# A gated cross-attention and FFN kernel whose key side runs one group further ahead

## The chip, the cores and the metric

One NeuronCore of a Trainium2 chip. The metric is the device time of one execution in microseconds (us), as the median of several runs. Engines: TensorE (PE; its weight loads are PEld), VectorE (DVE), ScalarE (ACT), GpSimd (POOL) and SyncE (SP), which issues most transfers. Every engine works through its own queue in order and waits on semaphores.

## What is computed

Sixteen batches of 128 rows x 256 features, with one attention head:

```
Q = layernorm(x) @ Wq.T + bq          K = ctx @ Wk.T + bk
P = softmax(mask(Q @ K.T))            over the 128 rows of ctx, no scaling
x1 = x + tanh(g_xattn) * (P @ ctx @ Wo.T + bo)
y  = layernorm(x1) @ sign(weights).T * scale + bias,  clipped to +-100
out = x1 + tanh(g_ffn) * y
```

All is float32. Inputs x and ctx are [16, 128, 256], weights 256 x 256.

## The kernel before, in words

Two batches form a group (GB = 2), so there are eight groups (G = 8), 0 to 7. The query and key weights are multiplied once, so that a group needs the scores of normalised x against K = ctx (WkWq) only, and Z = ctx Wo^T takes the place of V. For a group the work is:

- TensorE transposes ctx into `ps_cT` and normalised x into `ps_xT` (`transpose_ctx`, `transpose_x`, L454, four each).
- ScalarE casts `ps_cT` to `cT_hi` (L183), and VectorE takes the rest as `cT_lo` (L360). ScalarE copies `ps_xT` to `xT` (L187).
- TensorE makes K and Z, each as 12 matmuls of hi and lo parts (`project_K`, `project_Z`, L459). ScalarE evicts them (L193, L198).
- TensorE makes the scores: one matmul adds the mask (L515), then four write the products (L520). VectorE takes the negated maximum (`nmax`, L370), ScalarE the exponentials (L204). TensorE transposes P (L528) into the same PSUM bank, ScalarE evicts it (L209), and `attend` multiplies it by Z (L539).
- VectorE turns `ps_O` into x1 (`residual`, L380), takes its statistics (`stats_x1`, L352, L356). TensorE transposes x1, ScalarE and VectorE split it (L213, L365), and `ffn` multiplies it by the sign weights (L459). VectorE scales (L388), GpSimd adds the bias and clips (L299, L303), VectorE adds x1 (`final`, L393), SyncE stores.

GpSimd also normalises x (`norm_x`, L281) from rstd and offset, made for units of one or two groups (`UNITS`, `offsets_x`, L266 to L272) from VectorE's statistics (`stats_x`, L342, L346), adds the output bias to x (`add_bo`, L293), and makes the rstd of x1 (`rstd_1s`, L286, L288).

The order on every engine is written out by hand, one loop over steps i on each. Nothing is scheduled at run time. In step i TensorE takes the scores of group i, the transposes of group i+1, x1 of group i-1, Z of group i, K of group i+1, P^T of group i, FFN of group i-1 and attend of group i. Ahead of the loop stand the combined weights and group 0's transposes and K. In step 0 the transposes of the centred sign weights (`w_cent`) stand in the place of the FFN. `cT_hi`, `cT_lo`, `xT`, `K_sb`, `Z_sb`, `p_sb` and `PT_sb` have two buffers, `xn` three; every PSUM tile has one.

Of the kernel before, what the change touches and what calls it, by code (L numbers as in the profile page):

```python
# [5 lines left out]
ALU = mybir.AluOpType  # L6
ACT = mybir.ActivationFunctionType
AX = mybir.AxisListType
F32 = mybir.dt.float32
F32R = mybir.dt.float32r  # L10
# [3 lines left out]
P = 128  # L14
# [7 lines left out]
def gated_xattn_ffn(nc, x, ctx, mask, g_xattn, g_ffn, wq, bq, wk, bk, wo, bo, w_ffn, scale_ffn, bias_ffn, out):  # L22
# [8 lines left out]
    DC = D // P  # L31
# [10 lines left out]

    UNITS = [(0, 2), (2, 4), (4, 8), (8, 12), (12, 16)]

    STATS_AT = {0: (2, 3), 1: (4, 5), 2: (6,), 3: (7,)}
    unit_of = lambda g: next(n for n, (lo, hi) in enumerate(UNITS) if lo <= g * GB < hi)

    with ExitStack() as stack:
        def sb(name, shape, dt=F32):
            return stack.enter_context(nc.sbuf_tensor(name, shape, dt))  # L50
# [30 lines left out]

        xn = sb("xn", [P, 3, GB, D])
        xT = sb("xT", [P, 2, DC, T])
        cT_hi, cT_lo = sb("cT_hi", [P, 2, DC, T], F32R), sb("cT_lo", [P, 2, DC, T], F32R)
        K_sb = sb("K_sb", [P, 2, DC, T])
        Z_sb = sb("Z_sb", [P, 2, GB, D])
        p_sb, PT_sb = sb("p_sb", [P, 2, GB, P]), sb("PT_sb", [P, 2, GB, P])
# [83 lines left out]
        def _(act):  # L171
# [8 lines left out]

            def evict_cT_hi(g):
                act.wait_ge(cT_prod, g + 1)
                nc.scalar.copy(cT_hi[:, g % 2], ps_cT).then_inc(cT_hi_done, 1)  # L183

            def evict_xT(g):
                act.wait_ge(xT_prod, g + 1)
# [44 lines left out]
            evict_xT(0)  # L231
            act.wait_ge(ps_bi_ready, 1)
            nc.scalar.activation(bi_g[:], o_bank[:, D:2 * D], ACT.Identity, scale=tanh_g[:, 1:2]).then_inc(bi_g_ready, 1)
            for i in range(G + 1):
                if i + 1 < G:
                    evict_cT_hi(i + 1)
                if i < G:
                    exp(i)
                if i >= 1:
                    evict_x1T_hi(i - 1)  # L240
                if i + 1 < G:
                    evict_xT(i + 1)
                if i < G:
                    evict_Z(i)
                    evict_PT(i)
                if i + 1 < G:
                    evict_K(i + 1)
                if i == 0:
                    act.wait_ge(ps_wT_ready, 1)
                    nc.scalar.copy(wT[:], ps_x1T).then_inc(wT_ready, 1)  # L250

        @block.gpsimd
        def _(pool):
# [63 lines left out]
                                    channel_multiplier=1).then_inc(mask_ready, 1)  # L317
            offsets_x(1)
            norm_x(1)
            pool.wait_ge(bo_g_ready, 1)  # L320
            for i in range(G + 2):
                if i < G:
                    add_bo(i)
                if i == 2:
                    pool.wait_ge(bi_g_ready, 1)
                    pool.wait_ge(clip_ready, 2)
                if i >= 2:
                    bias_and_clip(i - 2)
                if i + 2 < G:
                    if unit_of(i + 2) != unit_of(i + 1):  # L330
                        offsets_x(unit_of(i + 2))
                    norm_x(i + 2)
                if 1 <= i <= G:
                    rstd_1s(i - 1)

        @block.vector
        def _(dve):
# [19 lines left out]

            def split_cT(g):
                dve.wait_ge(cT_hi_done, g + 1)
                nc.vector.tensor_tensor(cT_lo[:, g % 2], ps_cT, cT_hi[:, g % 2].bitcast(F32), ALU.subtract  # L360
                                        ).then_inc(cT_lo_done, 1)

            def split_x1T(g):
# [38 lines left out]
            for c in range(DC):  # L402
# [13 lines left out]
            dve.wait_ge(woT_hi_ready, 1)  # L416
            nc.vector.scalar_tensor_tensor(out=woT_lo[:], in0=ps_Z, scalar=tanh_g[:, 0:1], in1=woT_hi[:].bitcast(F32),
                                           op0=ALU.mult, op1=ALU.subtract).then_inc(woT_lo_ready, 1)
            for i in range(G + 2):
                if 1 <= i <= G:  # L420
                    residual(i - 1)
                if i < G:
                    max_of_scores(i)
                if i >= 2:
                    scale_ffn_out(i - 2)
                if i == 0:
                    dve.wait_ge(w_loaded, 16)
                    nc.vector.tensor_scalar(w_sign2[:], w_sb[:], 0.0, 2.0, ALU.is_ge, ALU.mult).then_inc(sign2_done, 1)
                    dve.wait_ge(sign2_done, 1)
                    nc.vector.tensor_reduce(w_sum[:], w_sign2[:], AX.X, ALU.add).then_inc(w_sum_done, 1)  # L430
                if i + 1 < G:
                    split_cT(i + 1)
                if i == 0:
                    dve.wait_ge(w_sum_done, 1)
                    nc.vector.tensor_scalar(w_mean[:], w_sum[:], 1.0 / D, None, ALU.mult).then_inc(w_mean_done, 1)
                    dve.wait_ge(w_mean_done, 1)
                    for c in range(DC):
                        nc.vector.tensor_scalar(w_cent[:, c], w_sign2[:, c], w_mean[:, c:c + 1], None, ALU.subtract
                                                ).then_inc(w_cent_ready, 1)
                if 1 <= i <= G:  # L440
                    stats_x1(i - 1)
                    split_x1T(i - 1)
                for g in STATS_AT.get(i, ()):
                    stats_x(g)
                if i >= 2:
                    final(i - 2)

        @block.tensor
        def _(pe):
# [32 lines left out]
            def project_K(g):  # L482
                pe.wait_ge(cT_lo_done, g + 1)
                if g >= 1:
                    pe.wait_ge(K_done, DC * g)
                else:
                    pe.wait_ge(wqk_lo_ready, 1)
                for m in range(DC):
                    pairs = []
                    for c in range(DC):  # L490
                        w_hi, w_lo = (w[:, c, m * P:(m + 1) * P] for w in (wqk_hi, wqk_lo))
                        pairs += [(w_hi, cT_hi[:, g % 2, c]), (w_hi, cT_lo[:, g % 2, c]), (w_lo, cT_hi[:, g % 2, c])]
                    last = accumulate(ps_K[:, m], pairs)
                last.then_inc(K_prod, 1)

            def project_Z(g):
                if g >= 1:
                    pe.wait_ge(Z_done, g)
                else:
                    pe.wait_ge(woT_lo_ready, 1)  # L500
                for b in range(GB):
                    pairs = []
                    for c in range(DC):
                        c_hi, c_lo = (t[:, g % 2, c, b * P:(b + 1) * P] for t in (cT_hi, cT_lo))
                        pairs += [(c_hi, woT_hi[:, c]), (c_hi, woT_lo[:, c]), (c_lo, woT_hi[:, c])]
                    last = accumulate(ps_Z[:, b], pairs)
                last.then_inc(Z_prod, 1)

            def scores(g):
                if g >= 1:  # L510
                    pe.wait_ge(PT_done, g)
                else:
                    pe.wait_ge(tanh_ready, 1)
                    pe.wait_ge(mask_ready, 1)
                nc.tensor.matmul(ps_S_both, ones_b[:], mask_sel[:, g].rearrange("p b k -> p (b k)"), start=True, stop=False)  # L515
                pe.wait_ge(xT_done, g + 1)
                pe.wait_ge(K_done, DC * (g + 1))
                for b in range(GB):
                    for c in range(DC):
                        last = nc.tensor.matmul(ps_S[b], xT[:, g % 2, c, b * P:(b + 1) * P],  # L520
                                                K_sb[:, g % 2, c, b * P:(b + 1) * P], start=False,
                                                stop=(b == GB - 1 and c == DC - 1))
                last.then_inc(S_prod, 1)

            def transpose_p(g):
                pe.wait_ge(p_done, GB * (g + 1))
                for b in range(GB):
                    last = nc.tensor.transpose(ps_PT[:, b], p_sb[:, g % 2, b], ident[:])  # L528
                last.then_inc(PT_prod, 1)
# [48 lines left out]
            transpose_x(0)  # L578
            pe.wait_ge(kbias_ready, 1)
            nc.tensor.matmul(o_bank[:, D:2 * D], ones_1[:], bi_row[:], start=True, stop=True).then_inc(ps_bi_ready, 1)  # L580
            for i in range(G + 1):
                if i < G:
                    scores(i)
                if i + 1 < G:
                    transpose_ctx(i + 1)
                if i >= 1:
                    transpose_x1(i - 1)
                if i + 1 < G:
                    transpose_x(i + 1)
                if i < G:  # L590
                    project_Z(i)
                if i + 1 < G:
                    project_K(i + 1)
                if i < G:
                    transpose_p(i)
                if i == 0:
                    pe.wait_ge(w_cent_ready, DC)
                    transposes(ps_x1T, w_cent).then_inc(ps_wT_ready, 1)
                else:
                    ffn(i - 1)  # L600
                if i < G:
                    attend(i)


# [25 lines left out]
```

## Time and profile before

| | us |
|---|---|
| median of 3 runs | 91.12 (89.64 to 91.77) |
| the profiled execution | 89.64, span 87.9 |
| TensorE busy | 74.0 (84%) |
| its weight loads | 66.5 (76%) |
| GpSimd busy | 58.7 (67%) |
| VectorE busy | 51.4 (58%) |
| ScalarE busy | 36.6 (42%) |

The span is what the profile shows from first to last record; the time of the execution is 1.74 us more. Busy shares are means over the whole span. In this kernel the first 18 us (loads and weights) and the last 12 (one group's way to the output) differ from the rest, so the stretches are read one by one. An idle engine matters only where another waits for it. The chain of waits gives matmuls the time until the next one starts, while the list of instructions gives each its full latency, so the same piece has a somewhat shorter time, and a start up to 0.1 us later, in the chain.

### The profile page before, as it was taken

The page shows a single profiled execution, that of the slowest core. Times are in us where ns is not written, and L with a number is a line of the kernel's source. Part 1 is how long each engine was busy: PE and PEld are TensorE (multiplying, and loading weights), DVE is VectorE, ACT ScalarE, POOL GpSimd, SP SyncE. Part 2 cuts the span into 40 slices and gives each one's busy share as a digit, 9 for nine tenths or more (in the row PEclk, how much of TensorE's full clock was granted, in tenths as well). Part 3 has the DMA queues.
Part 4 walks back from the last instruction along what each step waited for, and adds up shares of the span by engine and source line. Part 5 has one row for each costly group of instructions (what it writes and reads, how often), then busy time and mean ns, then how long its engine had stood idle before and what let it go on. Part 6 is the DMA issues. An engine that isn't in the chain of part 4 may idle for free.

```text
span 87.9 us, 1571 instructions
## 1 busy us (share of the span) xinstructions
PE 74.0 (84%) x528; PEld 66.5 (76%) x528; DVE 51.4 (58%) x151; ACT 36.6 (42%) x98; POOL 58.7 (67%) x105
## 2 busy tenths in 40 slices
PE   2993999989999999999999999999999996725000
PEld 2992778968979989997997999799799895514000
DVE  0039007509945947983993892596389078495330
ACT  0060306458356651951755395095257517020000
POOL 5000884592079970888999698899999909658740
PEclk9999858999999999999999999999999999999655
DMA  2899999900000000003003003000300300110303
GB/s 15 307 324 366 348 348 348 329 11 0 0 0 0 0 0 0 11 0 127 0 0 119 0 7 118 1 0 0 119 7 0 119 0 0 65 54 0 119 0 119
DMA packets 7697, 7.44 MB, mean 85 GB/s; under 512 B 775, under 2 KB 7434, under 8 KB 7690
## 3 DMA queue, kind: packets, MB, share of 16 engines
q1 hardware_dynamic: 7216, 7.08, 25.2%
q10 hardware_dynamic: 474, 0.27, 1.1%
q8 instruction: 4, 0.07, 0.3%
q14 instruction: 3, 0.02, 0.1%
HBM read 5.25 MB, written 2.10 MB: 84 GB/s over the span
## 4 chain that ended last, share of the span: by engine, by line
PE 68%; DVE 8%; DMA 5%; POOL 5%; ACTq 4%; issue 3%; ACT 2%; POOLq 1%; DVEq 0%
PE ps_K L459 17%; PE ps_S L520 10%; PE ps_Z L459 9%; PE ps_O L539 8%; PE ps_F L459 8%; DMA bi_row<-in_L_ffn_bias_dram 5%; PE ps_cT L454 4%; PE ps_x1T L454 3%; PE ps_xT L454 3%; POOL f_biased L299 3%; DVE f_scaled L388 2%; PE ps_S L528 2%; PE ps_S L515 2%; DVE cT_lo L360 1%; ACT K_sb L193 1%
## 5 line engine op out<-in xcount | busy, mean ns | idle before, releaser
L299 POOL TENSOR_TENSOR f_biased<-f_scaled,bi_g 128x256 f32<-128x256 f32 x16 | 11.4, 735 | 8.2 <-DVE f_scaled L388 8.2
L380 DVE SCALAR_TENSOR_TENSOR x_sb<-ps_O,recip_p,xb_sb 128x256 f32<-128x256 f32 x16 | 7.0, 479 | 12.3 <-PE ps_O L539 10.1
L293 POOL TENSOR_TENSOR xb_sb<-x_sb,bo_g 128x256 f32<-128x256 f32 x16 | 11.3, 729 | 0.0
L183 ACT CAST cT_hi<-ps_cT 128x512 fp32r<-128x512 f32 x8 | 4.7, 586 | 15.5 <-PE ps_cT L454 15.5
L459 PE MATMUL ps_F<-wT,x1T_hi 128*128 128x256 f32 x32 | 8.6, 303 | 2.3 <-DVE x1T_lo L365 2.3
L266 POOL TENSOR_SCALAR ve_x<-mv_x 128x4 f32<-128x4 f32 (+1 forms) x5 | 1.5, 292 | 12.9 <-DVE mv_x L346 12.8
L281 POOL TENSOR_SCALAR xn<-x_sb,rstd_x,off_x 128x256 f32<-128x256 f32 x16 | 9.7, 614 | 0.5
L459 PE MATMUL ps_Z<-woT_hi,cT_hi 128*128 128x256 f32 x32 | 9.6, 299 | 0.0
L520 PE MATMUL ps_S<-K_sb,xT 128*128 128x128 f32 x64 | 9.3, 288 | 0.3 <-ACT xT L187 0.3
L459 PE MATMUL ps_K<-cT_hi,wqk_hi 128*128 128x256 f32 x32 | 9.2, 287 | 0.2
L459 PE MATMUL ps_K<-cT_hi,wqk_lo 128*128 128x256 f32 x32 | 9.0, 282 | 0.0
L459 PE MATMUL ps_K<-cT_lo,wqk_hi 128*128 128x256 f32 x32 | 9.0, 282 | 0.0
L520 PEld LDWEIGHTS ps_S<-K_sb,xT 128*128 128x128 f32 x64 | 7.7, 191 | 1.5 <-ACT xT L187 0.7
L459 PE MATMUL ps_Z<-woT_lo,cT_hi 128*128 128x256 f32 x32 | 8.9, 277 | 0.0
L459 PE MATMUL ps_Z<-woT_hi,cT_lo 128*128 128x256 f32 x32 | 8.9, 277 | 0.0
L539 PE MATMUL ps_O<-Z_sb,PT_sb 128*128 128x256 f32 x32 | 8.3, 382 | 0.0
L459 PEld LDWEIGHTS ps_F<-wT,x1T_hi 128*128 128x128 f32 x32 | 6.0, 188 | 2.8 <-DVE x1T_lo L365 2.8
L459 PE MATMUL ps_F<-wT,x1T_lo 128*128 128x256 f32 x32 | 8.0, 282 | 0.0
L393 DVE TENSOR_TENSOR out_sb<-f_clip,x_sb 128x512 f32<-128x512 f32 x8 | 5.5, 692 | 3.8 <-POOL f_clip L303 3.8
L388 DVE SCALAR_TENSOR_TENSOR f_scaled<-ps_F,rstd,sc_g 128x256 f32<-128x256 f32 x16 | 7.0, 476 | 0.9 <-POOL rstd L288 0.9
L193 ACT ACTIVATE K_sb<-ps_K,kbias 128x256 f32<-128x256 f32 x16 | 6.7, 477 | 1.2 <-PE ps_K L459 1.2
L204 ACT ACTIVATE p_sb<-ps_S,nmax 128x128 f32<-128x128 f32 x16 | 5.8, 369 | 2.5 <-DVE nmax L370 2.5
(90 smaller groups left out, 194.5 us busy)
## 6 DMA issues: line engine op xcount, KB each, us to landing
ctx_sb<-in_ctx_dram SPq DMA_DIRECT2D x8, 256.0 KB, 6.6
x_sb<-in_x_dram SPq DMA_DIRECT2D x8, 256.0 KB, 6.4
out_dram<-out_sb SPq DMA_DIRECT2D x8, 256.0 KB, 2.1
wk_sb<-in_L_xattn_Wk_dram ACTq DMA_DIRECT2D x1, 256.0 KB, 3.9
wq_sb<-in_L_xattn_Wq_dram SPq DMA_DIRECT2D x1, 256.0 KB, 3.7
wo_sb<-in_L_xattn_Wo_dram SPq DMA_DIRECT2D x1, 256.0 KB, 4.8
w_sb<-in_L_ffn_weights_dram SPq DMA_DIRECT2D x1, 256.0 KB, 5.6
bq_col<-in_L_xattn_bq_dram ACTq DMA_DIRECT2D x1, 1.0 KB, 4.5
```

The lines of the kernel that those rows point to most:

```text
L193: nc.scalar.activation(K_sb[:, g % 2, c], ps_K[:, c], ACT.Identity, bias=kbias[:, c:c + 1]).then_inc(K_done, 1)
L204: nc.scalar.activation(p_sb[:, g % 2, b], ps_S[b], ACT.Exp, bias=nmax[:, r:r + 1], accum_out=psum_p[:, r:r + 1]).then_inc(p_done, 1)
L281: nc.gpsimd.tensor_scalar(xn[:, g % 3, b], x_sb[:, r], rstd_x[:, r:r + 1], off_x[:, r:r + 1], ALU.mult, ALU.add).then_inc(xn_done, 1)
L293: nc.gpsimd.tensor_tensor(xb_sb[:, r], x_sb[:, r], bo_g[:], ALU.add).then_inc(xb_done, 1)
L299: nc.gpsimd.tensor_tensor(f_biased[:, r], f_scaled[:, r], bi_g[:], ALU.add).then_inc(f_biased_done, 1)
L380: nc.vector.scalar_tensor_tensor(out=x1_sb[:, r], in0=ps_O[:, b], scalar=recip_p[:, r:r + 1], in1=xb_sb[:, r], op0=ALU.mult, op1=ALU.add). ...
L388: nc.vector.scalar_tensor_tensor(out=f_scaled[:, r], in0=ps_F[:, b], scalar=rstd_1[:, r:r + 1], in1=sc_g[:], op0=ALU.mult, op1=ALU.mult).t ...
L393: nc.vector.tensor_tensor(out_sb[:, rows(g)], f_clip[:, g % 2], x1_sb[:, rows(g)], ALU.add).then_inc(out_done, 1)
L454: last = nc.tensor.transpose(dst[:, c, b * P:(b + 1) * P], src[:, b, c * P:(c + 1) * P], ident[:])
L459: last = nc.tensor.matmul(dst, lhsT, rhs, start=(n == 0), stop=(n == len(pairs) - 1))
L520: last = nc.tensor.matmul(ps_S[b], xT[:, g % 2, c, b * P:(b + 1) * P], K_sb[:, g % 2, c, b * P:(b + 1) * P], start=False, stop=(b == GB - ...
L539: last = nc.tensor.matmul(ps_O[:, b], PT_sb[:, g % 2, b], Z_sb[:, g % 2, b], start=True, stop=True)
```

## The change

TensorE makes the scores of group 0, the transposes of group 1 and K of group 1 ahead of its loop. In step i it then takes the scores of group i+1, the transposes and K of group i+2, and, as before, Z, P^T and attend of group i and x1 and FFN of group i-1. The other engines' loops follow. `cT_hi` and `cT_lo` have three buffers. The scores of group g wait for the eviction of P^T of group g-2, and P^T of group i waits until the exponentials of group i+1 have read the bank. VectorE's statistics of x for groups 2 and 3 come ahead of the loop, and GpSimd normalises x one group further ahead. In the last step (i = 7) P^T comes first, then Z, x1 of group 6 and attend; the FFN of group 6, x1 and FFN of group 7 follow. In the last round VectorE splits x1 before its statistics.

```diff
-    STATS_AT = {0: (2, 3), 1: (4, 5), 2: (6,), 3: (7,)}
+    STATS_AT = {0: (4,), 1: (5,), 2: (6, 7)}
...
-        cT_hi, cT_lo = sb("cT_hi", [P, 2, DC, T], F32R), sb("cT_lo", [P, 2, DC, T], F32R)
+        cT_hi, cT_lo = sb("cT_hi", [P, 3, DC, T], F32R), sb("cT_lo", [P, 3, DC, T], F32R)
...
ScalarE
+            exp(0)
+            evict_cT_hi(1)
+            evict_xT(1)
+            evict_K(1)
             for i in range(G + 1):
+                if i + 2 < G:
+                    evict_cT_hi(i + 2)
                 if i + 1 < G:
-                    evict_cT_hi(i + 1)
-                if i < G:
-                    exp(i)
+                    exp(i + 1)
+                if i == G - 1:
+                    evict_PT(i)
+                    evict_Z(i)
                 if i >= 1:
                     evict_x1T_hi(i - 1)
-                if i + 1 < G:
-                    evict_xT(i + 1)
-                if i < G:
+                if i + 2 < G:
+                    evict_xT(i + 2)
+                if i < G - 1:
                     evict_Z(i)
                     evict_PT(i)
-                if i + 1 < G:
-                    evict_K(i + 1)
+                if i + 2 < G:
+                    evict_K(i + 2)
...
GpSimd
             norm_x(1)
+            offsets_x(2)
+            norm_x(2)
...
-                if i + 2 < G:
-                    if unit_of(i + 2) != unit_of(i + 1):
-                        offsets_x(unit_of(i + 2))
-                    norm_x(i + 2)
+                if i + 3 < G:
+                    if unit_of(i + 3) != unit_of(i + 2):
+                        offsets_x(unit_of(i + 3))
+                    norm_x(i + 3)
...
VectorE
+            max_of_scores(0)
+            split_cT(1)
+            stats_x(2)
+            stats_x(3)
             for i in range(G + 2):
                 if 1 <= i <= G:
                     residual(i - 1)
-                if i < G:
-                    max_of_scores(i)
+                if i + 1 < G:
+                    max_of_scores(i + 1)
...
-                if i + 1 < G:
-                    split_cT(i + 1)
+                if i + 2 < G:
+                    split_cT(i + 2)
...
-                if 1 <= i <= G:
+                if 1 <= i < G:
                     stats_x1(i - 1)
                     split_x1T(i - 1)
+                if i == G:
+                    split_x1T(i - 1)
+                    stats_x1(i - 1)
...
TensorE
             def scores(g):
-                if g >= 1:
-                    pe.wait_ge(PT_done, g)
+                if g >= 2:
+                    pe.wait_ge(PT_done, g - 1)
+                elif g == 1:
+                    pe.wait_ge(p_done, GB)
...
             def transpose_p(g):
-                pe.wait_ge(p_done, GB * (g + 1))
+
+                pe.wait_ge(p_done, GB * min(g + 2, G))
...
+            scores(0)
+            transpose_ctx(1)
+            transpose_x(1)
+            project_K(1)
+            for i in range(G):
                 if i + 1 < G:
+                    scores(i + 1)
+                if i + 2 < G:
+                    transpose_ctx(i + 2)
+                if 1 <= i < G - 1:
                     transpose_x1(i - 1)
+                if i + 2 < G:
+                    transpose_x(i + 2)
+                if i == G - 1:
                     transpose_p(i)
+                project_Z(i)
+                if i + 2 < G:
+                    project_K(i + 2)
+                if i < G - 1:
+                    transpose_p(i)
+                else:
+                    transpose_x1(i - 1)
...
+                elif i < G - 1:
                     ffn(i - 1)
+                attend(i)
+            ffn(G - 2)
+            transpose_x1(G - 1)
+            ffn(G - 1)
```

TensorE at the start, from the scores of group 0 on (`ps_S<-K_sb,xT` is the scores, `ps_cT` and `ps_xT` the transposes). Before:

```order
L515 MATMUL ps_S<-mask_sel,ones_b 128x258
L520 MATMUL ps_S<-K_sb,xT 128x128 x4
L454 MATMUL ps_cT<-ident,ctx_sb 128x128 x4
L454 MATMUL ps_xT<-ident,xn 128x128 x4
L459 MATMUL ps_Z<-woT_hi,cT_hi 128x256
```

Now:

```order
L533 MATMUL ps_S<-mask_sel,ones_b 128x258
L538 MATMUL ps_S<-K_sb,xT 128x128 x4
L470 MATMUL ps_cT<-ident,ctx_sb 128x128 x4
L470 MATMUL ps_xT<-ident,xn 128x128 x4
L475 MATMUL ps_K<-cT_hi,wqk_hi 128x256
```

The 12 matmuls of Z(0), which stood between the transposes of group 1 and K(1), come behind the next scores and transposes, and K(1) comes right behind the transposes that it needs.

ScalarE at the same place, behind the last of the bias rows (`bi_g`). Before:

```order
L233 ACTIVATE bi_g<-ps_O,tanh_g 128x256
L183 CAST cT_hi<-ps_cT 128x512
L204 ACTIVATE p_sb,psum_p<-ps_S,nmax 128x128 x2
L187 COPY xT<-ps_xT 128x512
L198 COPY Z_sb<-ps_Z 128x512
```

Now:

```order
L233 ACTIVATE bi_g<-ps_O,tanh_g 128x256
L204 ACTIVATE p_sb,psum_p<-ps_S,nmax 128x128 x2
L183 CAST cT_hi<-ps_cT 128x512
L187 COPY xT<-ps_xT 128x512
L193 ACTIVATE K_sb<-ps_K,kbias 128x256 x2
```

The exponentials of group 0 now stand ahead of the cast of group 1's cT, and the eviction of K(1) comes ahead of Z(0).

VectorE in its last rounds, from the x1 of group 7 on (`ps_F` is the FFN). Before:

```order
L380 SCALAR_TENSOR_TENSOR x_sb<-ps_O,recip_p,xb_sb 128x256 x2
L388 SCALAR_TENSOR_TENSOR f_scaled<-ps_F,rstd,sc_g 128x256 x2
L352 BN_STATS bn<-x_sb 128x6 x2
L356 BN_AGGR mv<-bn 128x2 x2
L365 TENSOR_TENSOR x1T_lo<-ps_x1T,x1T_hi 128x512
```

Now:

```order
L389 SCALAR_TENSOR_TENSOR x_sb<-ps_O,recip_p,xb_sb 128x256 x2
L397 SCALAR_TENSOR_TENSOR f_scaled<-ps_F,rstd,sc_g 128x256 x2
L374 TENSOR_TENSOR x1T_lo<-ps_x1T,x1T_hi 128x512
L361 BN_STATS bn<-x_sb 128x6 x2
L365 BN_AGGR mv<-bn 128x2 x2
```

The split of x1 has moved ahead of its statistics.

## Rows read from the trace of the kernel before

**Rows 1.** Stretches: start:end, length, busy us of each engine, clock, DMA.

```profile
10.00:14.00 4.00, 4.00 (x16) 3.31 (x15) 0.33 (x1) 1.45 (x4) 3.65 (x6) 0.57 1.10 348
18.39:25.34 6.95, 6.83 (x51) 6.01 (x51) 4.69 (x16) 4.17 (x12) 2.71 (x5) 1.00 0.01 2
32.96:40.42 7.46, 7.46 (x60) 6.95 (x60) 5.66 (x17) 3.95 (x11) 4.51 (x9) 1.00 0.07 22
70.26:76.48 6.22, 5.48 (x40) 4.67 (x39) 4.31 (x12) 2.15 (x7) 3.68 (x6) 1.00 0.00 0
```

**Rows 2.** The chain that ended last: start us, us, what.

```profile
13.86 0.59 ACT cT_hi L183
...
14.48 0.70 DVE cT_lo L360
...
15.23 1.71 PE ps_K L459 x12
...
17.02 0.84 ACT K_sb L193 x2
...
18.39 1.17 PE ps_S L520 x8
...
19.59 0.43 DVE nmax L370
...
21.89 1.70 PE ps_K L459 x12
...
25.40 0.21 PE ps_S L515
...
26.70 0.44 PE ps_cT L454 x4
...
27.58 0.59 PE ps_xT L454 x4
28.17 1.39 PE ps_Z L459 x12
29.56 1.43 PE ps_K L459 x12
...
70.33 0.21 PE ps_S L515
```

**Rows 3.** ScalarE in order of time, around the exponentials of group 7.

```profile
72.13 0.37 ACT L204 ACTIVATE p_sb<-ps_S,nmax 128x128 f32<-128x128 f32 x1 [2.47 <-DVE nmax L370]
...
72.83 0.58 ACT L213 CAST x1T_hi<-ps_x1T 128x512 fp32r<-128x512 f32 x1
```

**Rows 4.** VectorE and GpSimd in order of time: statistics and xn of group 2.

```profile
22.48 0.75 DVE L342 BATCH_NORM_STATS2 bn_x<-x_sb 128x6 f32<-128x256 f32 x2
...
24.39 0.19 POOL L266 TENSOR_SCALAR ve_x<-mv_x 128x4 f32<-128x4 f32 x1 [4.16 <-DVE mv_x L346]
...
26.36 1.09 POOL L281 TENSOR_SCALAR xn<-x_sb,rstd_x,off_x 128x256 f32<-128x256 f32 x2
```

**Rows 5.** VectorE, GpSimd and ScalarE after the last attend, in order of time.

```profile
76.60 0.88 DVE L380 SCALAR_TENSOR_TENSOR x_sb<-ps_O,recip_p,xb_sb 128x256 f32<-128x256 f32 x2 [0.95 <-PE ps_O L539]
77.39 0.86 DVE L388 SCALAR_TENSOR_TENSOR f_scaled<-ps_F,rstd,sc_g 128x256 f32<-128x256 f32 x2
...
78.22 0.58 ACT L213 CAST x1T_hi<-ps_x1T 128x512 fp32r<-128x512 f32 x1 [3.88 <-PE ps_x1T L454]
...
79.46 0.77 POOL L303 TENSOR_SCALAR f_clip<-f_biased,clip_hi,clip_lo 128x512 f32<-128x512 f32 x1
...
81.82 0.88 DVE L388 SCALAR_TENSOR_TENSOR f_scaled<-ps_F,rstd,sc_g 128x256 f32<-128x256 f32 x2 [0.87 <-POOL rstd L288]
...
84.68 0.69 DVE L393 TENSOR_TENSOR out_sb<-f_clip,x_sb 128x512 f32<-128x512 f32 x1 [1.99 <-POOL f_clip L303]
```

**Rows 6.** The list of waits: engine, line, waited for: us in total, times, longest.

```profile
PEld ps_S L515 <- issue: 2.3, 7, 0.3
...
PE ps_F L563 <- DMA bi_row<-in_L_ffn_bias_dram: 1.3, 1, 1.3
```

More of the change, by code:

```diff
@@ L182, in evict_cT_hi @@
                 act.wait_ge(cT_prod, g + 1)
-                nc.scalar.copy(cT_hi[:, g % 2], ps_cT).then_inc(cT_hi_done, 1)
+                nc.scalar.copy(cT_hi[:, g % 3], ps_cT).then_inc(cT_hi_done, 1)
             def evict_xT(g):
@@ L359, in split_cT @@
                 dve.wait_ge(cT_hi_done, g + 1)
-                nc.vector.tensor_tensor(cT_lo[:, g % 2], ps_cT, cT_hi[:, g % 2].bitcast(F32), ALU.subtract
+                nc.vector.tensor_tensor(cT_lo[:, g % 3], ps_cT, cT_hi[:, g % 3].bitcast(F32), ALU.subtract
                                         ).then_inc(cT_lo_done, 1)
@@ L491, in project_K @@
                         w_hi, w_lo = (w[:, c, m * P:(m + 1) * P] for w in (wqk_hi, wqk_lo))
-                        pairs += [(w_hi, cT_hi[:, g % 2, c]), (w_hi, cT_lo[:, g % 2, c]), (w_lo, cT_hi[:, g % 2, c])]
+                        pairs += [(w_hi, cT_hi[:, g % 3, c]), (w_hi, cT_lo[:, g % 3, c]), (w_lo, cT_hi[:, g % 3, c])]
                     last = accumulate(ps_K[:, m], pairs)
@@ L503, in project_Z @@
                     for c in range(DC):
-                        c_hi, c_lo = (t[:, g % 2, c, b * P:(b + 1) * P] for t in (cT_hi, cT_lo))
+                        c_hi, c_lo = (t[:, g % 3, c, b * P:(b + 1) * P] for t in (cT_hi, cT_lo))
                         pairs += [(c_hi, woT_hi[:, c]), (c_hi, woT_lo[:, c]), (c_lo, woT_hi[:, c])]
@@ L580, in _ @@
             nc.tensor.matmul(o_bank[:, D:2 * D], ones_1[:], bi_row[:], start=True, stop=True).then_inc(ps_bi_ready, 1)
-            for i in range(G + 1):
-                if i < G:
-                    scores(i)
+            scores(0)
[3 more added lines that the diff above has]
+            for i in range(G):
                 if i + 1 < G:
-                    transpose_ctx(i + 1)
-                if i >= 1:
+                    scores(i + 1)
+                if i + 2 < G:
+                    transpose_ctx(i + 2)
+                if 1 <= i < G - 1:
                     transpose_x1(i - 1)
[L588 to L594, printed above, removed]
-                    transpose_p(i)
+                if i + 2 < G:
+                    transpose_x(i + 2)
+                if i == G - 1:
+                    transpose_p(i)
+                project_Z(i)
[5 more added lines that the diff above has]
+                    transpose_x1(i - 1)
                 if i == 0:
@@ L598, in _ @@
                     transposes(ps_x1T, w_cent).then_inc(ps_wT_ready, 1)
-                else:
+                elif i < G - 1:
                     ffn(i - 1)
-                if i < G:
-                    attend(i)
+                attend(i)
+            ffn(G - 2)
+            transpose_x1(G - 1)
+            ffn(G - 1)
 _INS = ['x', 'ctx_1024', 'mask_BxS2_bk0', 'g_xattn', 'g_ffn', 'L0_xattn_Wq', 'L0_xattn_bq', 'L0_xattn_Wk', 'L0_xattn_bk',
```

## The prediction, made before the change was run

> **What bounds the kernel now.** I read the stretches first, then the chain of waits, then single engines. In the stretches [rows 1] a middle step lasts 7.46 us; TensorE is busy through all of it, its weight loads for 6.95, VectorE for 5.66 and ScalarE for 3.95, at a granted clock of 1.00. From 18.39 to 25.34 TensorE has 0.12 us of idle. So from 18.39 to about 71 the kernel is a queue of matmuls without holes, and a step that starts earlier does not make that queue shorter. Holes are only before 18.39, in the last full step (6.22 us with 5.48 busy) and after it, where TensorE waits for others until the span ends at 87.9. The change can win only there, and it can lose wherever TensorE is made to wait between 18 and 71.
>
> **The head.** Until the scores of group 0 end at 19.56 [rows 2] nothing moves. Now TensorE has the transposes of ctx and x of group 1 to do, and then the key projection K(1), which needs cT_lo(1). Before, Z(0), 1.39 us of matmuls, stood between and hid that chain. Now nothing does, and the chain itself is longer, since on ScalarE the exponentials of group 0 come ahead of the eviction of cT. Step by step, with spacings from the same pairs elsewhere:
> - The maximum ends at 20.02 [rows 2], and the exponentials follow at 20.05. They hold ScalarE 0.70 (72.13 to 72.83 in [rows 3]), so cT_hi(1) starts at 20.75.
> - From cT_hi to cT_lo is 0.62, from cT_lo to the first matmul of K 0.75 [rows 2]: K(1) at 22.12. Before it was 21.89, with Z(0) already done. Loss so far 0.23 + 1.39 = 1.6 us.
> - The scores of group 1 need K(1) out of PSUM. From the start of K(0) to its eviction is 1.79, the eviction is 0.84, and 0.04 to the matmul [rows 2]: 24.79. Before, the step's other work lay over this. Now TensorE has only the mask matmul (0.21), so it loses some 0.7.
> - The scores take 1.17, to 25.96, the transposes of ctx(2) 0.44, to 26.40. The transposes of x(2) wait for xn(2). VectorE reaches the statistics of groups 2 and 3 behind cT_lo(1), at 21.37 + 0.70 = 22.07. From there GpSimd starts 1.91 later, its first xn another 1.97 later and both take 1.09 [rows 4]: 27.04, and the transposes start at 27.10, another 0.7 lost.
> - With 0.59 for them and 1.39 for Z(0), K(2) starts at 29.08 [rows 2]. Its cT_lo is behind the sign work of w on VectorE as before (K(1) began 21.89 - 19.56 = 2.3 us after the scores, so 28.3) and is ready. From K to the mask matmul that opens the next step is 25.40 - 21.89 = 3.51, less 0.27 because K now follows work (1.43 for 1.70): 32.32.
>
> The middle steps keep 7.46, as the work in one is the same and VectorE and ScalarE have more room, not less. What is late next would be GpSimd: xn(4) needs the statistics of group 5, which VectorE now takes in step 1; by the spacings above it stands about 1 us ahead of need. So step 6 begins at 32.32 + 5 x 7.46 = 69.62.
>
> **The tail.** Step 6 of the change has the very pieces that step 7 had before (scores of the last group, transposes of x1, Z, P^T, FFN, attend), and began then at 70.33 [rows 2]. So it is 0.71 early, and its attend(6) ends at 76.48 - 0.71 = 75.77. But before, that was attend(7), and only a tail followed. Now group 7 has P^T, Z and attend still to come, with the x1 of group 6 and FFN(6). In the account of TensorE: a group's part that stays back is 7.46 less the part drawn forward (0.21 + 1.17 + 0.44 + 0.44 + 1.43 = 3.7), so 3.8; 3.8 - 0.7 = 3.1 us is what the head costs.
> - P^T(7) (half of a 0.44 set of transposes) and Z(7) 1.39 end at 77.4, the eviction of Z 0.6 later, attend(7) 78.0 to 79.1.
> - On VectorE x1(6) starts at 76.60 - 0.71 = 75.89, f_scaled(5) 0.79 later, 76.68, and the clip on GpSimd 2.07 behind it (79.46 - 77.39), 78.75 to 79.52 [rows 5]. VectorE takes out_sb(5) (0.69) before x1(7): with 0.1 for the reciprocal, an estimate, x1(7) starts at 80.35, not at 79.2. Attend(7) ahead of FFN(6) therefore buys little: VectorE's own queue is what comes last.
> - f_scaled(6) follows at 81.14 (0.79; GpSimd's rstd, 2.36 behind the clip, gives 81.11), its clip starts at 83.21 and ends at 83.98. x1T_hi(7) is 1.62 behind x1(7) (78.22 - 76.60), 81.97, x1T_lo 0.62 later, 82.59, and now the statistics of x1(7) come behind it: 0.70 + about 0.9 (half of the 1.91 of two groups), 84.2, and 0.1 to GpSimd. Before, the statistics lay under the wait for x1T_hi. GpSimd's rstd(7) took up to 1.59 after a clip (81.82 - 79.46 - 0.77), less when it has waited (its first piece is 0.19 in [rows 4]): f_scaled(7) between 84.9 and 85.6, taken 85.3.
> - From f_scaled(7) to the end of the span is 87.9 - 81.82 = 6.08: 91.4.
>
> **The sum.** Span 91.4 for 87.9: +3.5 us. The profiled execution took 89.64, so 93.1 in its terms. It is the lowest of three runs shown (median 91.12, mean 90.84, 1.2 above it). The runs of the change should scatter alike, so I forecast **94.3**. What a measurement can tell from no change is about 2%, 1.8 us; the middle of the forecast lies well over it. Bounds of the single terms: the head at least 1.6 (K(1) alone), at most 3.1 + 0.5; the tail's residual at best 1.1 earlier (if GpSimd clips sooner), at worst 0.6 later.
>
> **Idle and weights.** A matmul row without holes need not be the floor. The row that bears on it is the weight loads' 6.95 of 7.46 us [rows 1], and 0.33 us of idle seven times ahead of the mask's weights, 2.3 in all [rows 6]. The matmuls on both sides show no idle, so I give this nothing in the sum. The Trainium skill, Perfetto Trace Analysis, section Identifying the Most-Contended Engine, says that matmul busy share is no good measure of the room left and that the share of weight loads is; by it there would be 0.51 us of room in a step, 3.1 in six.
>
> **Rivals.**
> 1. *The period falls.* The scores' wait is now for a P^T evicted one step earlier. If it is the freshness of that wait that holds the mask's weights back, 0.33 x 7 = 2.3 us come back: 93.1 - 2.3 = 90.8 in the profile's terms, 92.0 in the median's, no change. It decides from 0.23 us a step (1.6 of 3.5). Against it: no matmul of a middle step is late. That is the one on the other side. 12%.
> 2. *The clock falls in the head.* TensorE stood idle 1.3 us before the matmuls of the bias rows [rows 6], ahead of 10 us; from 10 to 14, though busy all through, it ran at a mean 0.57, in good part at 1.2 GHz and not 2.4 [rows 1]. The change puts waits of 1.7, 0.7 and 0.7 us into 20 to 27. A stretch like that costs 4 x (1 - 0.57) = 1.7: 94.8, or 96.0 in the median's terms. Against it: with a wait of 0.7 in the last full step, the clock stayed at 1.00. 13%. The Trainium skill, TensorE: Matmul & The Clock Gate, Part 1, calls half rate the default that activity lifts; this trace agrees, at 0.57 after the idle start.
> 3. *The head is hidden.* If TensorE finds its operands in the head (the change does not do what I say there), the 3.1 go, and the tail alone leaves +0.4: 90.0, or 91.2, no change; with the residual 1.1 earlier 88.9, or 90.1, just under 2% faster at the best. Against it: all spacings are from rows. 12%, of which half is faster by over 2% with an error in the tail of the same sign.
>
> The forecast itself has 63%. So slower by over 2%: 0.63 + 0.13 less a little for its low end, 0.75; within 2%: 0.18; faster: 0.07. The range from 91.6 to 96.2 takes in rivals 1 and 2 and the bounds of head and tail, and leaves out rival 3 and what is slower than rival 2.
>
> **What would show it.** In the changed profile: K(1) at about 22.1 with 1.7 us of TensorE idle ahead of it, charged to cT_lo; scores(1) near 24.8 behind an idle charged to K_sb; transposes of x(2) behind xn near 27.1; the third mask matmul at 32.3; then steps of 7.46, the last scores near 69.6 and the last f_scaled at 85.3. Steps under 7.2 us would be rival 1, a clock below 1.00 after 20 rival 2, a third mask matmul before 30.5 rival 3. I am wrong on the tail if x1(7) starts right behind attend(7).

## The result and the profile after

The changed kernel takes 95.24 us (median of 4, 94.86 to 95.71), the kernel before 90.87 on the same chip: the ratio is 1.058 (95% interval 1.052 to 1.064). It is slower, as forecast; 94.3 was forecast, with 91.6 to 96.2 as the range. The profiled execution took 94.86 with a span of 93.0, against 89.64 and 87.9: +5.1 us in the span for the +3.5 of the sum.

Stretches of the changed kernel (start:end, length, busy us of PE, PEld, DVE, ACT, POOL, clock, DMA), to set beside [rows 1]:

```profile
10.00:14.00 4.00, 4.00 (x19) 3.56 (x18) 0.98 (x2) 1.98 (x4) 3.62 (x6) 0.65 1.10 348
14.00:18.00 4.00, 4.00 (x20) 4.00 (x21) 2.03 (x6) 0.85 (x2) 2.60 (x7) 0.50 1.00 315
20.71:33.65 12.94, 9.60 (x72) 8.20 (x70) 7.16 (x22) 6.63 (x19) 6.93 (x12) 1.00 0.01 1
41.11:48.57 7.46, 7.46 (x60) 6.95 (x60) 6.57 (x21) 3.96 (x11) 7.10 (x12) 1.00 0.02 4
```

The step is 7.46 us as before, with the same weight loads. From the end of the scores of group 0 to the third mask matmul TensorE is idle for 12.94 - 9.60 = 3.3 us. And before 18 us, where TensorE has the same work in both programs, the changed kernel's clock stands at 1.2 GHz from 14 to 18; in the profile of the kernel before it was back at 2.4 GHz from 14 us on.

The chain of the changed kernel (start us, us, what), beside [rows 2]:

```profile
19.54 1.17 PE ps_S L538 x8
...
20.73 0.44 DVE nmax L379
...
21.20 0.81 ACT p_sb L204 x4
22.00 0.48 ACT cT_hi L183
...
22.51 0.69 DVE cT_lo L369
23.20 0.66 DVE bn_x L351 x2
...
26.98 1.34 POOL xn L288 x2
...
28.37 0.66 PE ps_xT L470 x4
29.02 1.38 PE ps_Z L475 x12
30.41 1.43 PE ps_K L475 x12
...
33.65 0.21 PE ps_S L533
...
70.95 0.21 PE ps_S L533
```

This is the chain of the prediction link by link: exponentials, cast, split, statistics, xn, and only then TensorE. The scores of group 0 start 1.15 us later than before. From there to the third mask matmul it is 33.65 - 19.54 = 14.11 us; the prediction said 32.32 - 18.39 = 13.93. The difference is mostly xn, 1.34 for 1.09: in this trace it runs while VectorE does the sign work of w, and where xn(2) runs without it (run 2) it takes 1.09.

TensorE's waits in the changed kernel (engine, line, waited for: total, times, longest):

```profile
PEld ps_S L533 <- issue: 2.0, 6, 0.3
...
PE ps_K L475 <- DVE cT_lo L369: 1.7, 1, 1.7
...
PE ps_S L538 <- ACT K_sb L193: 0.9, 1, 0.9
...
PE ps_xT L470 <- POOL xn L288: 0.8, 1, 0.8
```

Of TensorE's own waits (the rows that begin with PE), 1.7, 0.7 and 0.7 were forecast, in these places and for these releasers.

The tail, VectorE and GpSimd in order of time:

```profile
78.01 0.87 DVE L397 SCALAR_TENSOR_TENSOR f_scaled<-ps_F,rstd,sc_g 128x256 f32<-128x256 f32 x2
...
80.88 0.69 DVE L402 TENSOR_TENSOR out_sb<-f_clip,x_sb 128x512 f32<-128x512 f32 x1 [0.36 <-POOL f_clip L310]
...
81.68 0.88 DVE L389 SCALAR_TENSOR_TENSOR x_sb<-ps_O,recip_p,xb_sb 128x256 f32<-128x256 f32 x2
82.48 0.87 DVE L397 SCALAR_TENSOR_TENSOR f_scaled<-ps_F,rstd,sc_g 128x256 f32<-128x256 f32 x2
...
85.41 0.66 DVE L402 TENSOR_TENSOR out_sb<-f_clip,x_sb 128x512 f32<-128x512 f32 x1
85.58 0.54 POOL L293 TENSOR_SCALAR ve<-mv 128x2 f32<-128x2 f32 x1 [0.27 <-DVE mv L365]
...
86.94 0.87 DVE L397 SCALAR_TENSOR_TENSOR f_scaled<-ps_F,rstd,sc_g 128x256 f32<-128x256 f32 x2 [0.87 <-POOL rstd L295]
```

x1(7) starts right behind out_sb(5), as said, and GpSimd waits 0.27 us for the statistics, which are now behind the split. The three f_scaled stand 4.47 and 4.46 apart; this even spacing comes back below.

### The profile page after: what moved, and what is told of

Same layout as the page of the kernel before. It is cut to its first block, busy times and chain, and to the rows that moved or that the text cites. A ratio compares the mean times of both kernels' runs of the same rounds, so it can differ in the third digit from the quotient of the medians.

```text
span 93.0 us, 1571 instructions
## 1 busy us (share of the span) xinstructions
PE 76.2 (82%) x528; PEld 68.6 (74%) x528; DVE 52.3 (56%) x151; ACT 36.8 (40%) x98; POOL 59.3 (64%) x105
## 4 chain that ended last, share of the span: by engine, by line
PE 61%; DVE 11%; POOL 8%; DMA 5%; issue 4%; ACT 3%; ACTq 3%; POOLq 1%; DVEq 0%
PE ps_K L475 15%; PE ps_Z L475 9%; PE ps_S L538 8%; PE ps_O L558 7%; PE ps_F L475 6%; DMA bi_row<-in_L_ffn_bias_dram 5%; PE ps_x1T L470 4%; PE ps_cT L470 3%; PE ps_xT L470 3%; POOL f_biased L306 2%; DVE f_scaled L397 2%; PE ps_O L475 2%; POOL xn L288 1%; DVE bn L361 1%; PE ps_S L547 1%
## 5 line engine op out<-in xcount | busy, mean ns | idle before, releaser
L475 PE MATMUL ps_K<-cT_hi,wqk_hi 128*128 128x256 f32 x32 | 9.8, 306 | 1.7 <-DVE cT_lo L369 1.7
L475 PE MATMUL ps_K<-cT_hi,wqk_lo 128*128 128x256 f32 x32 | 9.6, 299 | 0.0
L475 PE MATMUL ps_K<-cT_lo,wqk_hi 128*128 128x256 f32 x32 | 9.5, 298 | 0.0
L475 PEld LDWEIGHTS ps_K<-cT_hi,wqk_hi 128*128 128x128 f32 x32 | 6.6, 207 | 1.9 <-DVE cT_lo L369 1.9
L379 DVE TENSOR_REDUCE nmax<-ps_S 128x2 f32<-128x258 f32 x8 | 3.4, 426 | 7.9 <-PE ps_S L538 7.9
```

What stands on the lines that cost most here:

```text
L379: nc.vector.tensor_reduce(nmax[:, rows(g)], ps_S_max, AX.X, ALU.max, negate=True).then_inc(nmax_done, 1)
L475: last = nc.tensor.matmul(dst, lhsT, rhs, start=(n == 0), stop=(n == len(pairs) - 1))
```

## The experiments

Two theories stood. **Order**: TensorE loses 3.1 us in the head to waits that Z(0) used to cover, and some tenths in the tail. **Clock**: part or all of it is the clock at the start. Two distances in a trace are free of the start: from the scores of group 0 to the third mask matmul ("head"; 14.1 us in the changed kernel), and from these scores to the end of the span ("rest"; 69.5 us in the kernel before, 73.5 in the changed one). The times of whole kernels carry the scatter of the start until it is removed, in the fifth run. Four of the later runs (zfill_warm, cast_first_warm, out_late_warm, stats_back_warm) were timed on another chip than the 92.44 us that they are set against; for them the rest, in the trace, is the firmer number.

**1. Z(0) back ahead of K(1)** (zfill)

```diff
ScalarE
+            evict_Z(0)
             evict_K(1)
...
TensorE
             transpose_x(1)
+            project_Z(0)
             project_K(1)
...
-                project_Z(i)
+                if i >= 1:
+                    project_Z(i)
...
```

> The changed kernel with Z(0) moved back between the transposes of group 1 and K(1) on TensorE, with its eviction ahead of K(1)'s on ScalarE. Theory (the head's loss is Z(0)'s lost cover and waits on chains): Z(0) fits the 1.7 us idle ahead of K(1), so K(1) starts as before, x(2)'s transposes still wait for xn(2), and then K(2) follows at once but for cT_lo(2): from the scores of group 0 to the third mask matmul 14.1 becomes 13.0 to 13.1, the time about 1.0 us less than the changed kernel (ratio to before about 1.045). Rival (the loss is only the clock at the start): no change in that distance, ratio as the changed kernel's 1.058.

Head 13.3 (34.73 - 21.42), rest 72.7 for 73.5. So 0.8 us came back, not the 1.0 expected: with Z(0) gone from its later place, K(2) waits for cT_lo(2), which VectorE makes behind the sign work (the signs of w, their sum and their mean). The time, 94.28 with a ratio of 1.036 (1.021 to 1.052), says little: in its profile the scores began at 21.42, 1.9 us later than in the changed kernel.

**2. Statistics of groups 2 and 3 ahead of the first maximum** (stats_early)

```diff
+            stats_x(2)
+            stats_x(3)
             max_of_scores(0)
             split_cT(1)
-            stats_x(2)
-            stats_x(3)
```

> The changed kernel with VectorE's statistics of x for groups 2 and 3 ahead of the maximum of scores 0, where VectorE is idle for 3.7 us. Theory: xn(2) is ready long before its transposes, the 0.8 us idle ahead of them goes, the rest of the head stays: 14.1 from the scores of group 0 to the third mask matmul becomes 13.3, time 0.8 us less, ratio about 1.048. Rival (clock only): 14.1 stays.

Head 13.3 (31.58 - 18.27), rest 72.7, and the wait for xn is gone. As expected by Order. The time is 93.19 us (92.79 to 96.12), a ratio of 1.034 (1.024 to 1.044); 1.048 was expected.

**3. Four repairs of the head** (head_all): Z(0) and statistics as above, and

```diff
-            exp(0)
             evict_cT_hi(1)
+            exp(0)
...
             project_K(1)
+            transpose_ctx(2)
+            transpose_x(2)
...
```

> The changed kernel with four repairs of its head: Z(0) ahead of K(1), statistics of groups 2 and 3 ahead of the first maximum, the cast of cT(1) ahead of the exponentials of group 0, and the transposes of group 2 ahead of the scores of group 1. Theory: TensorE has no hole left in the head: from the scores of group 0 to the third mask matmul 14.1 becomes 10.9 (7.0 as before for the first step, 0.2+1.1+0.9+1.4 = 3.6 for the pieces drawn forward, 0.3), the time falls by 3.1 us, ratio about 1.02, and what is left of the slowdown is the tail's 0.4 to 0.7 us and the clock at the start. Rival (a queue that runs one group ahead is worth something once its head is free): ratio under 0.99. Rival (clock only): 1.058.

Not as expected: the head is 14.2 and not 10.9, and the time 95.20 us (93.15 to 95.36), no better than the changed kernel's. VectorE reached cT_lo(2) late behind the sign work, TensorE stood 2.15 us from 27.10 to 29.25, and the clock fell; K(2) took 2.92 us for its usual 1.43 to 1.70. So the run says nothing on what a head without holes is worth. Stretches of this kernel:

```profile
26.00:29.00 3.00, 1.08 (x8) 0.89 (x8) 1.85 (x4) 1.56 (x6) 1.47 (x3) 1.00 0.00 0
29.00:33.00 4.00, 3.75 (x18) 3.58 (x18) 1.82 (x9) 0.36 (x2) 0.00 (x0) 0.57 0.00 0
```

That is rival 2 in another kernel: 1.08 us of work in three at full clock, then a mean clock of 0.57. In the changed kernel itself the waits were 1.7, 0.9 and 0.8 us (9.60 us of work in 12.94) and the clock stayed at 1.00.

**4. The tail's order alone, in the kernel before** (before_tail)

```diff
-                else:
+                elif i != G - 1:
                     ffn(i - 1)
                 if i < G:
                     attend(i)
+                if i == G - 1:
+                    ffn(i - 1)
```

> The kernel before, with one part of the change alone: attend(7) ahead of FFN(6) in the last full step. Theory: attend(7) starts at 74.4 in place of 75.5, x1(7) on VectorE at 75.6 in place of 76.6 (behind out_sb(5)), all of the tail 0.85 us earlier, ratio about 0.991. Rival (GpSimd's queue bounds the tail, so the order on TensorE buys nothing): last f_scaled unmoved, ratio 1.00.

Rest 68.5 for 69.5: 1.0 us for the 0.85 expected by the theory. Median 89.37 against 90.77, within the scatter of both.

**5. The hole before the bias rows filled, in the kernel before** (before_warm)

```diff
+            for _ in range(12):
+                nc.tensor.transpose(ps_x1T[:, 0, 0:P], ident[:], ident[:])
             pe.wait_ge(rows_loaded, 48)
```

> The kernel before with 12 transposes of the identity more, between the gate's matmul and the wait for the bias rows, where TensorE is idle 1.1 to 1.3 us. Theory (the scatter of the runs, 88.0 to 92.7, is a stretch at 1.2 GHz between 9 and 18 us that comes at another place and length in each execution, and follows that idle): with the hole filled the clock stays at 1.00 to the first scores, these start at 17 us or before (18.4 in the profile before), all runs fall near 88 and scatter under 1 us. Rival (the matmuls that use little of the array bring the clock down, or chance does): the stretch at 1.2 GHz stays and so does the scatter.

88.48 us, all six runs between 88.33 and 88.81, ratio 0.986 (0.984 to 0.989), while 16 runs of the kernel before on the same chip lay between 89.51 and 92.15. Its stretch from 9 to 18:

```profile
9.00:18.00 9.00, 8.43 (x55) 6.96 (x55) 2.93 (x9) 4.45 (x10) 7.57 (x16) 1.00 1.08 340
```

The clock is 1.00 throughout and the scores start at 17.19. In the six profiles without the 12 transposes it was down somewhere between 8.6 and 20 us and the scores started between 18.27 and 21.42; in all eight with them it was 1.00 from 9 to 18 and they started between 17.03 and 17.51. The rest is 69.5 as before.

**6. The same in the changed kernel** (after_warm)

> The changed kernel with the same 12 transposes. Theory: as the kernel before with them plus 3.9 us, which the order costs (3.1 in the head, 0.4 to 0.8 in the tail); 14.1 from the scores of group 0 to the third mask matmul. Rival (part of the measured 5.2 us comes from the change setting off the clock's fall at the start): the distance to the kernel before with them is what is left, still 3.9 by the trace, but the other kernels' scatter stays.

92.44 us (92.22 to 92.74), against 88.48 on the same chip: +3.96 us, a ratio of 1.045 (1.038 to 1.050 between the extremes of the runs). The rest is 73.5 for 69.5. So the order costs 4.0 us. Of the +5.1 between the first two profiles the other 1.15 stands ahead of the scores of group 0, where the clock was low for longer; that the 0.4 by which the medians' +4.4 exceeds 4.0 has the same source is likely, but no trace of those runs shows it.

**7. A head without holes** (head_full_warm): the repairs of 3, the 12 transposes, and on VectorE the sign work of w ahead of the first maximum and the split of cT(2) ahead of the second.

```diff
             stats_x(2)
             stats_x(3)
+            dve.wait_ge(w_loaded, 16)
+            nc.vector.tensor_scalar(w_sign2[:], w_sb[:], 0.0, 2.0, ALU.is_ge, ALU.mult).then_inc(sign2_done, 1)
...
             max_of_scores(0)
             split_cT(1)
+            dve.wait_ge(w_sum_done, 1)
+            nc.vector.tensor_scalar(w_mean[:], w_sum[:], 1.0 / D, None, ALU.mult).then_inc(w_mean_done, 1)
...
+            split_cT(2)
```

> The changed kernel with the 12 transposes and a head without holes: Z(0) ahead of K(1), cast of cT(1) ahead of the exponentials of group 0, statistics of groups 2 and 3 and the sign work of w ahead of the first maximum, transposes of group 2 ahead of the scores of group 1, and the split of cT(2) ahead of the second maximum. Theory: from the scores of group 0 to the third mask matmul 10.6 to 10.9 in place of 14.1, so the order costs nothing in the head, and what is left to the kernel before with the 12 transposes is the tail, 0.4 to 0.9 us, ratio between them 1.005 to 1.01. Rival (to run ahead is worth something by itself): under 0.99 of the kernel before with the 12 transposes.

89.03 us (88.66 to 89.57), ratio to the kernel before 0.991 (0.988 to 0.994), to the kernel before with the 12 transposes 1.006. The head is 10.55:

```profile
17.43 1.16 PE ps_S L539 x8
18.59 0.44 PE ps_cT L471 x4
19.03 0.44 PE ps_xT L471 x4
19.46 1.38 PE ps_Z L476 x12
20.84 1.44 PE ps_K L476 x12
22.28 0.44 PE ps_cT L471 x4
22.71 0.44 PE ps_xT L471 x4
23.15 0.21 PE ps_S L534
23.36 1.13 PE ps_S L539 x8
24.49 1.68 PE ps_K L476 x12
...
27.98 0.21 PE ps_S L534
```

TensorE's pieces follow each other without a wait of more than 0.3 us. 3.4 us of the 4.0 are gone in the time, 3.5 in the trace. The queue still runs one group ahead, and that alone is worth nothing: the rest is 70.0, 0.5 above the kernel before. The 0.5 stands behind the head: from the third mask matmul to the end of the span it is 59.4 us in both this kernel and the changed one, so the repairs touched nothing there.

**8. Tail order and transposes together, in the kernel before** (before_tail_warm)

> The kernel before with attend(7) ahead of FFN(6) and the 12 transposes. Theory: both gains add, 1.0 us for the order in the last step and what the transposes give by themselves (1 to 2 us against the median), so near 87 to 88, ratio 0.965 to 0.975. Rival (the clock's stretch comes by chance): 0.985 to 0.99 as with the tail alone.

87.68 us (87.44 to 87.81), ratio 0.976 (0.974 to 0.979): faster than both kernels, and at the edge of the 0.965 to 0.975 expected. The rest is 68.9, so the tail's order gives 0.6 us here, 1.0 in run 4, and 0.8 in the time. What separates the two traces is the clock in the tail: it was 0.50 from 78 us on in this one and 1.00 in run 4, and here the last f_scaled waits for FFN(7), not for GpSimd's rstd:

```profile
77.79 0.58 PE L459 MATMUL ps_F<-wT,x1T_hi 128*128 128x256 f32 x1 [1.68 <-DVE x1T_lo L365]
...
79.97 0.88 DVE L388 SCALAR_TENSOR_TENSOR f_scaled<-ps_F,rstd,sc_g 128x256 f32<-128x256 f32 x2 [1.00 <-PE ps_F L459]
```

**9 and 10. The head's pieces with the clock held** (zfill_warm: the edit of 1; cast_first_warm: the first edit of 3 alone)

> The changed kernel with the 12 transposes and Z(0) moved back ahead of K(1). Theory (the head's loss is Z(0)'s cover plus two waits): from the scores of group 0 to the third mask matmul 14.1 becomes 13.3, as in the run without the transposes, with the rest of Z(0)'s 1.39 lost to the wait for cT_lo(2) behind the sign work; time 92.4 becomes 91.6. Rival (the waits move and nothing is won): 92.4.

> The changed kernel with the 12 transposes and the cast of cT(1) ahead of the exponentials of group 0 on ScalarE. Theory: the chain cT_hi, cT_lo, K(1) starts 0.7 to 0.8 us earlier, all behind it too (the statistics of groups 2 and 3 follow cT_lo(1)), 14.1 becomes 13.3 to 13.4, time 91.7. Rival (the exponentials are what comes last for K(1)'s successors): 92.4.

91.62 and 91.58 us for 92.44: 0.8 and 0.9 us. (One of the four runs of cast_first_warm took 94.15; the median does not rest on it, but the 12 transposes are no guarantee.) The rests are 72.7 and 72.8 for 73.5: 0.8 and 0.7.

**11. out_sb(5) behind x1(7)** (out_late_warm)

```diff
                 if 1 <= i <= G:
                     residual(i - 1)
+                if i == G:
+                    final(i - 3)
...
-                if i >= 2:
+                if i >= 2 and i != G - 1:
                     final(i - 2)
```

> The changed kernel with the 12 transposes and out_sb(5) behind x1(7) on VectorE. Theory 1 (as predicted: VectorE's own queue, out_sb(5) ahead of x1(7), is what comes last in the tail): x1(7) starts at 78.6 in place of 79.7 and all behind it 0.9 to 1.1 earlier, time 91.4. Theory 2 (GpSimd's ring of bias, clip and rstd, 4.46 us from one f_scaled to the next, is the bound): x1(7) starts earlier, f_scaled(6) stays at 80.46 and f_scaled(7) at 84.7 to 84.9, time 92.2 to 92.4.

92.07 (91.83 to 92.31), 0.4 less. Its tail, VectorE and GpSimd in order of time:

```profile
78.42 0.88 DVE L389 SCALAR_TENSOR_TENSOR x_sb<-ps_O,recip_p,xb_sb 128x256 f32<-128x256 f32 x2
78.71 0.19 POOL L293 TENSOR_SCALAR ve<-mv 128x2 f32<-128x2 f32 x1
78.98 0.71 POOL L295 TENSOR_TENSOR rstd<-ve,half 128x2 f32<-128x2 f32 x1
79.22 0.68 DVE L402 TENSOR_TENSOR out_sb<-f_clip,x_sb 128x512 f32<-128x512 f32 x1
79.81 0.87 DVE L397 SCALAR_TENSOR_TENSOR f_scaled<-ps_F,rstd,sc_g 128x256 f32<-128x256 f32 x2
...
82.68 0.69 DVE L402 TENSOR_TENSOR out_sb<-f_clip,x_sb 128x512 f32<-128x512 f32 x1 [0.44 <-POOL f_clip L310]
82.73 0.69 POOL L293 TENSOR_SCALAR ve<-mv 128x2 f32<-128x2 f32 x1
...
84.25 0.88 DVE L397 SCALAR_TENSOR_TENSOR f_scaled<-ps_F,rstd,sc_g 128x256 f32<-128x256 f32 x2 [0.87 <-POOL rstd L295]
```

x1(7) came 1.05 us earlier when both are counted from the scores of group 0 (61.11 for 62.16), f_scaled(6) and f_scaled(7) only 0.45 and 0.47. Between the two it is still 4.44. Neither theory has it whole. In the profile of run 6 two things kept f_scaled(6) back and ended within 0.1 us of each other: VectorE's queue (x1(7) right ahead of it) and GpSimd's rstd(6), done at 80.39 with f_scaled(6) at 80.46. The edit moved both. rstd(6) came early because its first piece (`ve`, 128x2) took 0.19 us in place of 0.69, and that goes with out_sb: where VectorE runs out_sb at the same time, this piece ends 0.05 us after out_sb (82.68 + 0.69 = 83.37, 82.73 + 0.69 = 83.42). So the 0.45 cannot be put down to VectorE's queue alone. What separates f_scaled(6) from f_scaled(7) is GpSimd, and some 0.5 of its 4.44 us is that delay beside out_sb(6). Whether moving out_sb(6) too would win it back was not tested.

**12. Statistics of x1(7) ahead of its split** (stats_back_warm)

```diff
-                if 1 <= i < G:
+                if 1 <= i <= G:
                     stats_x1(i - 1)
                     split_x1T(i - 1)
-                if i == G:
-                    split_x1T(i - 1)
-                    stats_x1(i - 1)
```

> The changed kernel with the 12 transposes and the statistics of x1(7) ahead of its split, as in the kernel before. Theory: the statistics fill VectorE's 0.6 us wait for x1T_hi(7), GpSimd finds mv(7) when its clip is done and not 0.3 us after, f_scaled(7) 0.1 to 0.3 earlier, time 92.1 to 92.4. Rival (FFN(7), now 0.25 later, is what f_scaled(7) waits for): 92.5 or more.

92.40 for 92.44. GpSimd's 0.28 us wait is gone, but its first piece takes 0.69 in place of 0.54. In both kernels it ends 0.05 us after out_sb(6) does (85.41 + 0.66 = 86.07 and 85.58 + 0.54 = 86.12 in the profile of the changed kernel), so its earlier start buys nothing, and f_scaled(7) comes 67.37 after the scores of group 0 for 67.41. This part of the change costs nothing.

## Why the prediction was right, and where it was not

- **Bound by TensorE, period unchanged.** Right: 7.46 us in every middle step before and after. Rival 1 is out: the mask's weights are still preceded by 0.3 us of idle (2.0 us in six), though the P^T they wait for is a step older. No run says what that 0.3 us is. By the rule of the Trainium skill, Perfetto Trace Analysis, Identifying the Most-Contended Engine, the weight loads' 6.95 of 7.46 left 0.5 us of room in a step; the step stayed at 7.46, but no run here was aimed at that room.
- **The head.** Right in its mechanism and nearly in its size. The sum said 13.93 us, the trace 14.11. Undone one at a time, Z(0), the statistics and the cast gave back 0.8, 0.8 and 0.7 to 0.9 us; all together, with the sign work moved, 3.5. Z(0) alone gave less than its 1.39, because the next wait (cT_lo(2)) took over, which the sum's first loss of 1.6, read as what Z(0) alone would give back, does not show.
- **The tail.** The size was near (the scores of group 0 to f_scaled(7): 67.4 in the trace, 85.3 - 18.39 = 66.9 in the sum; of the 0.5, 0.2 is the head and 0.3 the last rstd). The reason given was half wrong. "VectorE's own queue is what comes last" is worth 0.45 us at most (run 11), and a part of GpSimd's moved with it. The other part is GpSimd's ring: bias, clip and two pieces of rstd take 4.4 to 4.5 us from one f_scaled to the next, in both kernels (81.82 - 77.39 = 4.43 before [rows 5]), and the change leaves two rounds of it after the last full step in place of one. An earlier attend(7) cannot shorten that. The sum had 85.3 - 81.14 = 4.16 for the last round, by taking GpSimd's rstd as shorter when it has waited; it was 4.46. The 0.19 of [rows 4] is what such a piece takes when VectorE is not at out_sb, whether GpSimd has waited or not. "The statistics come behind it" was taken as a cost and is none (run 12).
- **The clock.** Rival 2, a fall in the head of the changed kernel, did not come: 1.00 from 20 to the last matmuls. What I left out of the sum is that the start, the same in both programs, differs from one execution to the next. The scores of group 0 began 1.15 us later in the profiled execution, which is most of the 1.6 by which the span overshot; what is left is 0.2 in the head and 0.3 in the tail. The 1.2 added for the median allowed for scatter without a cause for it, and that it about covered the later start is luck: the changed kernel's profiled execution was the lowest of its four, too, and yet 1.8 above the 93.1 of the sum. In the tail the clock did fall in run 6 (0.67 from 82 to 84), at no cost there, since f_scaled(7) waited for rstd; in run 8 it did cost. The sum had no term for it.
- **Rival 3**, the head hidden, was not what happened, but run 7 bears out its arithmetic: it had +0.4 for a tail alone, +0.5 was found.

## What to carry to other kernels

Where one engine's queue has no holes, running a chain further ahead cannot make it shorter; it only moves holes to the place where the pipeline fills, and there, in this kernel, each piece taken out uncovered a wait. Before pulling work forward, list for the first two rounds what lies over each hand-over between engines, and move with it everything that the pulled work needs (here the cast, the statistics and the sign work). Measure the rest of the kernel from a fixed event behind the start when the start scatters, or remove the scatter first: the 12 spare transposes made 4.0 us readable from four runs.

## What the runs showed of the hardware

- The scatter of this kernel, 88.0 to 92.7 us over 17 runs on one chip (mean clock 0.980 in the shortest, 0.909 in the longest), goes with TensorE's clock at the start. TensorE worked from 1.7 us to between 7.3 and 7.8, in some profiles with a wait of up to 0.95 us for the gate row, then stood for 1.1 to 1.3 us before the bias rows, and in six of six profiles the clock was at 1.2 GHz for some us between 8.6 and 20. With that hole filled by transposes, it was at 2.4 GHz from 9 to 18 in eight of eight, and of the 45 runs of these eight kernels 43 stayed within 0.5 us of their kernel's median (the two others were 0.54 and 2.57 off). The Trainium skill, TensorE: Matmul & The Clock Gate, Part 4, says that the full clock does not engage for the transpose mode; here the filling was transposes and the clock stayed up, though no trace shows whether they ran in that mode.
- The granted clock in the profile is not to be relied on ahead of its first change. It reads 1.00 from 0 us on, but the 24 transposes from 1.70 us on took 5.38 us in run 5, 0.22 each, while four of them take 0.44 us later, 0.11 each. By that pace the array ran at the lower level through most of them.
- A wait of 2.15 us in run 3 was followed by a mean clock of 0.57 over 4 us and about doubled K(2) (2.92 us); waits of 1.7, 0.9 and 0.8 us with work between them were not.
- GpSimd's small piece of rstd (`ve` and `ve_x`, 2 or 4 columns) takes 0.19 to 0.20 us in 107 of its 182 instances in the 14 profiles. In the other 75, VectorE runs out_sb (two operands of 128x512) at the time, and the piece takes 0.50 to 0.69 and ends 0.04 to 0.06 us after out_sb. xn, 1.09 otherwise, took 1.33 to 1.34 beside the signs of w, 1.22 to 1.24 beside w_cent and up to 1.63 beside out_sb. So an instruction of VectorE can lengthen one of GpSimd, and where it stands in VectorE's queue is part of GpSimd's time.
